# Two more delta tiles of the last stage handed from VectorE to ScalarE and GpSimd (tiles 4 and 6)

## The reference, cut to what matters

```
logits = flat @ router_w.T
topk_vals, topk_idx = jax.lax.top_k(logits, TOP_K)
...
gates = jax.nn.softmax(sparse, axis=-1)
mid = jnp.einsum('tf,erf->ter', flat, A)
all_deltas = jnp.einsum('ter,eor->teo', mid, B) * LORA_SCALE
delta = jnp.einsum('te,teo->to', gates, all_deltas)
...
x = _layernorm(x + delta)
```

## Time and profile before

| | us |
|---|---|
| median of 3 runs | 990.43 |
| lowest, highest | 989.28, 991.11 |
| the profiled execution's own time | 990.58 |
| span of the profiled execution | 988.4 |
| its time outside the span | 2.18 |

### The profile page before, as it was taken

One profiled execution on the slowest core, in us unless ns is written; L12 is line 12 of the kernel. 1 busy time (PEld: TensorE's weight loads), 2 busy tenths in 40 slices (PEclk: granted clock), 3 DMA queues, 4 the chain that ended last, 5 costly groups with the idle time before them and its releaser, 6 DMA issues.

```text
span 988.4 us, 15661 instructions
## 1 busy us (share of the span) xinstructions
PE 948.0 (96%) x4926; PEld 785.0 (79%) x4926; DVE 638.7 (65%) x1421; ACT 486.6 (49%) x1358; POOL 524.1 (53%) x432
## 2 busy tenths in 40 slices
PE   5998999999999999989999999999999999999895
PEld 3766688878888888878888888888888888888782
DVE  5745553422312257888768778778768778778877
ACT  5756442322231246645645644654645645555554
POOL 4336533743433456864575574673673763854323
PEclk9999999999999999999999999999999999999997
DMA  6200123310111111010110110110110120110002
GB/s 221 86 1 1 42 62 112 107 64 0 64 64 64 43 65 35 23 43 22 44 44 22 43 53 11 42 53 11 42 54 10 42 64 0 43 53 12 1 1 85
DMA packets 18024, 45.69 MB, mean 46 GB/s; under 512 B 2176, under 2 KB 2816, under 8 KB 16704
## 3 DMA queue, kind: packets, MB, share of 16 engines
q1 hardware_dynamic: 17984, 45.20, 13.8%
HBM read 43.10 MB, written 2.10 MB: 46 GB/s over the span
## 4 chain that ended last, share of the span: by engine, by line
PE 75%; POOL 8%; DVE 7%; issue 4%; ACT 2%; DMA 2%; SPq 0%; POOLq 0%; DVEq 0%; ACTq 0%
PE bank L511 22%; PE bank L512 21%; PE bank L513 21%; PE bank L828 4%; POOL w_lo L1580 2%; PE bank L838 2%; DMA raw_a<-in_w_q 2%; DVE pb L2299 1%; POOL pb L1837 1%; POOL res L1698 1%; PE bank L522 1%; POOL raw_a L1742 1%; PE bank L815 1%; DVE bst L2129 1%; PE bank L572 1%
## 5 line engine op out<-in xcount | busy, mean ns | idle before, releaser
L511 PE MATMUL bank<-act_hi,w_hi 128*128 128x512 f32 x448 | 183.6, 410 | 1.6 <-DVE act_lo L1942 1.6
L512 PE MATMUL bank<-act_lo,w_hi 128*128 128x512 f32 x448 | 175.6, 392 | 0.0
L513 PE MATMUL bank<-act_hi,w_lo 128*128 128x512 f32 x448 | 175.5, 392 | 0.0
L1837 POOL TENSOR_TENSOR pb<-pb,prec 128x512 f32<-128x512 f32 x64 | 66.8, 1044 | 163.2 <-DVE prec L2308 163.2
L1580 POOL TENSOR_TENSOR w_lo<-raw_a,w_hi 128x512 fp32r<-128x512 f32 x101 | 130.2, 1301 | 37.1 <-ACT w_hi L1302 21.6
L1371 ACT ACTIVATE pb<-pb,nmax 128x128 f32<-128x128 f32 x256 | 99.4, 391 | 46.5 <-DVE nmax L2303 46.4
L511 PE MATMUL bank<-w_hi,ot_hi 128*128 128x512 f32 x256 | 106.2, 415 | 1.1 <-DVE ot_lo L1942 0.6
L1580 POOL TENSOR_TENSOR h_lo<-hb,h_hi 128x512 fp32r<-128x512 f32 x28 | 37.4, 1336 | 120.5 <-ACT h_hi L1243 120.5
L511 PEld LDWEIGHTS bank<-act_hi,w_hi 128*128 128x128 f32 x448 | 84.9, 190 | 20.5 <-issue 4.4
L513 PE MATMUL bank<-w_hi,ot_lo 128*128 128x512 f32 x256 | 100.5, 393 | 0.0
L512 PE MATMUL bank<-w_lo,ot_hi 128*128 128x512 f32 x256 | 100.2, 391 | 0.0
(11 more groups left out here) (233 smaller groups left out, 2328.3 us busy)
## 6 DMA issues: line engine op xcount, KB each, us to landing
raw_a<-in_w_gu SPq DMA_DIRECT2D x7, 1024.0 KB, 5.3
raw_a<-in_w_q SPq DMA_DIRECT2D x28, 256.0 KB, 3.3
raw_b<-in_w_kv SPq DMA_DIRECT2D x8, 512.0 KB, 3.3
raw_b<-in_w_dn SPq DMA_DIRECT2D x7, 512.0 KB, 3.5
raw_b<-in_w_o SPq DMA_DIRECT2D x7, 512.0 KB, 5.0
raw_a<-in_w_o SPq DMA_DIRECT2D x14, 256.0 KB, 4.0
res<-in_x SPq DMA_DIRECT2D x8, 256.0 KB, 6.1
raw_b<-in_ctx_t SPq DMA_DIRECT2D x8, 256.0 KB, 3.0
```

Source lines behind the costliest of these rows:

```text
L511: mm(o, l_hi, r_hi, start=first, stop=False)
L512: mm(o, l_hi, r_lo, start=False, stop=False)
L513: return mm(o, l_lo, r_hi, start=False, stop=last)
L1837: TT(pb[:, jj % 2, :, :], pb[:, jj % 2, :, :], prec[:, jj % 2, :].unsqueeze(2).to_broadcast([P, GH, L]), ALU.mult).then_inc(p_norm, 1)
```

## The change

`BY_POOL` becomes (0, 2, 4, 6). Tiles 4 and 6 are copied by ScalarE and added by GpSimd, as tiles 0 and 2 were; VectorE's two additions of these tiles go, and a wait on `dl_pool`, GpSimd's count of finished additions, stands in their place. The two buffers in `xn` are used in turn, so a copy of tile 4 waits until GpSimd has read tile 0's. ScalarE's copy of tile 4 stands between its reads of the second and third group's transposes, its copy of tile 6 behind `last_norm(2)`. GpSimd's addition of tile 4 stands behind `rsqrt(33)` (tile 0), that of tile 6 behind `rsqrt(35)` (tile 3).

```
-        BY_POOL = (0, 2)
+        BY_POOL = (0, 2, 4, 6)
...
                 act.wait_ge(dl_mm, BY_POOL[k] + 1)
-                A(xn[:, k, :], bank[DL_BANK[BY_POOL[k]]][:, :], ACT.Copy).then_inc(dl_cp, 1)
+                if k >= 2:
+                    act.wait_ge(dl_pool, k - 1)
+                A(xn[:, k % 2, :], bank[DL_BANK[BY_POOL[k]]][:, :], ACT.Copy).then_inc(dl_cp, 1)
...
             mt_evac(1)
+            dl_copy(2)
             mt_evac(2)
             for b in FIN[:7]:
                 last_norm(b)
+                if b == 2:
+                    dl_copy(3)
...
-                TT(res[:, b, :], res[:, b, :], xn[:, k, :], ALU.add).then_inc(dl_pool, 1)
+                TT(res[:, b, :], res[:, b, :], xn[:, k % 2, :], ALU.add).then_inc(dl_pool, 1)
...
             for i in range(33, 40):
                 rsqrt(i)
+                if i in (33, 35):
+                    dl_sum((i - 29) // 2)
...
             for b in range(4, B):
-                add_delta(b)
+                if b in BY_POOL:
+                    dve.wait_ge(dl_pool, BY_POOL.index(b) + 1)
+                else:
+                    add_delta(b)
                 last_mean(b - 1)
                 ln_stats(32 + b)
```

## The result

| | before | changed |
|---|---|---|
| median | 990.52 us (22 runs) | 991.87 us (22 runs) |
| lowest, highest | 988.81, 991.49 | 989.66, 993.13 |
| ratio to before, 95% interval | | 1.0012 [1.0006, 1.0017] |
| span of the profiled execution | 988.4 us | 989.5 us |

The changed kernel is slower by 0.12%, by the interval 0.6 to 1.7 us; the medians lie 1.35 us apart, and 0.8 us was forecast.

A forecast was written before the change was run, and what follows sets the result against it. VectorE's 1.90 us turns were taken as bound by the chain variance, GpSimd's root, `mr`, not by the additions. 0.31 + 0.50 - 0 = +0.81 us on 990.43 gave 991.24, told as 991.2; range 990.1 to 992.3.

The forecast's parts named there:

- The removed additions: VectorE's additions of tiles 4 and 6, hidden behind GpSimd's root: gain 0, at most 0.14 us together.
- Tile 4's term: GpSimd's addition of tile 4 holds up the root of tile 2, starting at 975.64 instead of 975.33: +0.31 us.
- Tile 6's term: GpSimd's addition of tile 6 holds up the root of tile 4, from 979.44 to 979.94: +0.50 us.
- The clock: TensorE's granted clock taken as unchanged: 1.00 up to 975.20, 0.51 behind it, so tile 6's delta takes 2.04 us.
- Rival 1: GpSimd's addition of tile 6 stops `mr` of tile 3 if the copy is done early: +1.29, 991.7 us; chance 18%.
- Rival 2: VectorE's additions are on the path, so removing two gives 0.68 each: -1.36, 989.1 us; chance 6%.
- Rival 3: Both GpSimd additions land before an `mr`, of tile 0 and of tile 3: +2.15, 992.6 us; chance 3%.
- the lesser case: Tile 6's copy comes so that neither root waits: +0.31 or less, 990.7 us; chance 13%.
- One reading of the prediction: The 128x1 row at 933.36, 0.15 us inside GpSimd's operation to 933.40, shows that this form isn't held.
- the 0.3 us that the prediction left out: Variance of tile 4 at 979.20 held to 979.98 by GpSimd's addition, its root to about 980.2: some 0.3 us more.

The follow-up runs named there:

- no_adds_4_6: Kernel before with the additions of tiles 4 and 6 left out, nothing in their place (output lacks these deltas): last VectorE instruction -0.15 us.
- tile4_only: Kernel before with tile 4 alone also handed to GpSimd, tile 6 still added by VectorE: last VectorE instruction +0.34 us.
- tile6_only: Kernel before with tile 6 alone also handed to GpSimd, tile 4 still added by VectorE: last VectorE instruction +0.83 us.
- tile4_late: Kernel before with tile 4 alone also handed over, GpSimd's addition of it behind the root of tile 2: last VectorE instruction +0.97 us.
- tile6_ahead: Kernel before with tile 6 alone also handed over, its delta (bank 0) directly behind tile 4's and its copy earlier: last VectorE instruction +0.97 us.
- mean_later: Kernel before with `mr` of tiles 2 to 6 behind the next tile's statistics: last VectorE instruction -0.58 us, ratio 1.0 [0.9992, 1.0009].
- mean_inside_pool: Changed kernel with `mr` between the next tile's two statistics steps, GpSimd's addition of tile 6 behind tile 4's root: ratio 0.9987 [0.9978, 0.9995].

## Why the prediction was right

**The removed additions** were put at a gain of 0, with 0.14 as the upper bound. In the changed kernel the turn without an addition is 1.90, gain 0. no_adds_4_6 measures the upper bound as 0.15, and shows where it lies: with the root's wait alone before `mr` a turn is 1.83. From the variance of tile 3 to its `mr` it is 0.81 there, with neither an addition nor a second wait, and 0.89 in the changed kernel, with no addition but two waits (978.52 - 977.63). So the double wait is worth 0.07, and the change keeps it by putting `dl_pool` in the place of `dl_add`.

**Tile 4's term**, 0.31: measured 0.34 in tile4_only and at `mr` of tile 2 in the changed kernel (976.62 - 0.30 = 976.32, forecast 976.29). The copy lasts 0.60 and not 0.58.

**Tile 6's term**, 0.50: this step was right in its time and wrong as a separate cost. The root of tile 4 was put at 979.94 and came at 979.96. But 0.50 is only what is left of it behind tile 4's 0.31, and tile6_only costs 0.83 by itself. The sum should have been written as the later of two times, tile 6's addition ending at 979.94 or the variance of tile 4, and not as two costs; undoing tile 4 alone, which by the prediction's sum brings 0.31, brings nothing.

**The clock** was taken as unchanged. In the four traces of the changed kernel it was, as far as the deltas of tiles 4 and 6 are concerned; that no early fall came into them is luck. The prediction missed that it is not assured: in the 14 traces it falls from 1.00 to 0.50, from 2.4 to 1.2 GHz, anywhere from 2.3 to 5.5 us behind the mark, under an instruction stream that is the same up to there for all kernels but those with a moved delta. In the trace of the kernel before, the chain behind the mark doesn't pass through these deltas.

**Rival 1** did not occur in the changed kernel (all its `mr` last 0.16) and occurs where its condition is met, in tile4_late and tile6_ahead, at +0.97; it was priced there at +0.99 and +1.0, and in the prediction, on top of tile 4's delay, at +1.29. **Rival 2**, -1.36, falls with no_adds_4_6. **Rival 3** did not occur in any of the four traces of the changed kernel and was not tested by itself; nor did the lesser case, in which neither root waits. The clock of tile 6's delta, on which rival 1 hung, was rightly read from the rows.

One reading of the prediction fails: the variance at 933.36 starts 0.04 us before the end of GpSimd's operation at 933.40 and runs on behind it, so it can't show that such an operation isn't held. The changed kernel shows it: the variance at 975.39 keeps its 0.15 us in the middle of GpSimd's addition from 974.74 to 976.00, and the one at 979.53 beside the addition from 979.04 to 980.30. So the 0.3 us that the prediction left out on that row's word were rightly left out.

**The size.** The stage's +0.83 lies inside the timed 0.6 to 1.7 us. The middle of that interval, 1.2, is higher. Some executions with an early clock would explain it, but no trace of the changed kernel shows one. The timed runs give a hint. Those of the changed kernel with a mean granted clock of 0.992 or more have a median of 990.35 us (5 runs), against 989.5 for such runs of the kernel before (14 of the 40 timed beside no_adds_4_6 and tile6_ahead): +0.8. At 0.988 and 0.989 it is 992.17 (15 runs) against 990.73 (22 runs): +1.4. The four traces with a mean clock of 0.992 or more fall late (4.7 us behind the mark or later), and the four early falls all have a lower one. But the two sides weren't timed together, and late falls occur at the lower mean clocks as well, so this stays open.

## What to carry to other kernels

Before moving work off an engine, look whether the chain passes through that work or only beside it; here 0.68 us of an addition hid behind a 0.9 us round trip of a 128x1 value through another engine, and moving the value's consumer behind the next tile's work brought the last instruction forward by 0.58 us, where moving two additions set it back by 0.83. An engine that answers small urgent requests is a poor place for a 1.26 us job. Here it delayed the request behind it, and where it started just ahead of a 128x1 VectorE operation with both inputs in SBUF, that lasted 1.14 us instead of 0.16. When two delays hit the same chain from different sources and the second has a time of its own, take the later of the two times, not their sum.

## What the hardware showed beyond the forecast

- TensorE's granted clock fell at 2.3 to 5.5 us behind the same instruction in 14 traces. A path that leads through TensorE near such a fall has two lengths here: 1.12 or 2.07 us for one delta.
- Two semaphores to wait for instead of one put 0.07 us on VectorE's `mr`, also when the one that was added had long been reached (dl_pool in the changed kernel).
- With the last two tiles finished 0.25 us apart (mean_later) the tail behind the last instruction's start is 3.46 us, with 1.32 us between them (before) or 0.65 (mean_inside_pool) it is 2.99. Each tile's output is one transfer of 256 KB, and the DMA rows (the last two numbers are the share of the DMA engines and GB/s) show where the 0.47 goes: before, in mean_later, and in mean_inside_pool.

```profile
986.40:986.75 0.35, 0.00 (x0) 0.00 (x0) 0.00 (x0) 0.00 (x0) 0.00 (x0) 0.50 0.00 0
986.80:987.40 0.60, 0.00 (x0) 0.00 (x0) 0.00 (x0) 0.00 (x0) 0.00 (x0) 0.50 0.96 365
```
```profile
986.85:987.45 0.60, 0.00 (x0) 0.00 (x0) 0.00 (x0) 0.00 (x0) 0.00 (x0) 0.50 0.92 345
987.45:988.15 0.70, 0.00 (x0) 0.00 (x0) 0.00 (x0) 0.00 (x0) 0.00 (x0) 0.50 1.01 380
```
```profile
986.10:986.70 0.60, 0.00 (x0) 0.00 (x0) 0.00 (x0) 0.00 (x0) 0.00 (x0) 0.50 1.03 386
```

Before, the DMA engines stand still and then carry tile 7 alone, from 986.8 to 987.5, so one transfer takes about 0.7 us. It starts about 0.85 behind the end of the tile's last operation. In mean_later the engines are full from 986.85 to about 988.3, 1.4 us for both tiles: by these numbers (an estimate) tile 7's could start at 987.1 and finds them busy with tile 6's until about 987.6. With 0.65 between the tiles, as in mean_inside_pool, the first is through when the second comes.
